# Idle products ahead of the first rows, an opening in another order, and gathered rows added by TensorE at the end

## What is computed

```python
def _L0_attn_ref(x, Wq, bq, Wkv, bkv, Wo):      # 8 query heads, one key/value head, sinusoidal positions
    scores = jnp.einsum('bhqd,bkd->bhqk', q, k) * scale
    scores = jnp.where(causal[None, None, :, :], scores, jnp.finfo(scores.dtype).min)
    probs = jax.nn.softmax(scores, axis=-1)
...
def _L0_ffn_ref(h, router_w, w1, b1, w2, b2):   # 14 experts, the best one, gelu
...
def _L1_attn_ref(x, W_in, W_delta, b_delta, W_B, W_C, A_log, D_param, W_out):
    def step(h, inp):                            # 256 channels x 16 states, over 1024 tokens
        d_t, B_t, C_t, u_t = inp
        dA = jnp.exp(d_t[..., None] * A)
        h = dA * h + d_t[..., None] * B_t[:, None, :] * u_t[..., None]
        y_t = jnp.einsum('bdn,bn->bd', h, C_t)
        return (h, y_t)
...
    y = jnp.swapaxes(ys, 0, 1) + u * D_param
    y = y * jax.nn.silu(res)
    return y @ W_out
def _L1_ffn_ref(x, gate_w, w1, w2):             # 8 experts, the best two, relu
    for e in range(NUM_EXPERTS):
        h = jax.nn.relu(jnp.einsum('bsd,fd->bsf', x, w1[e]))
        y = jnp.einsum('bsf,df->bsd', h, w2[e])
        out = out + combine[..., e, None] * y
    return out

xn = _layernorm(x, axis=-1)
x = x + _L0_attn_ref(xn, ...) + _L0_ffn_ref(xn, ...)
xn = _layernorm(x, axis=-1)
x = x + _L1_attn_ref(xn, ...) + _L1_ffn_ref(xn, ...)
```

## Time and profile before

| what | us |
|---|---|
| median of 3 runs (lowest, highest) | 730.55 (729.79, 736.21) |
| the profiled execution | 729.45 |
| its span, first to last instruction | 727.6 |
| DVE busy | 531.4 (73%) |
| TensorE busy | 636.8 (88%) |
| ScalarE busy | 417.7 (57%) |
| POOL busy | 251.3 (35%) |
| TensorE's mean granted clock | 0.958 |

### The profile page before, as it was taken

One profiled execution on the slowest core, in us unless ns is written; L12 is line 12 of the kernel. 1 busy time (PEld: TensorE's weight loads), 2 busy tenths in 40 slices (PEclk: granted clock), 3 DMA queues, 4 the chain that ended last, 5 costly groups with the idle time before them and its releaser, 6 DMA issues. The chain is left out here.

```text
span 727.6 us, 11182 instructions
## 1 busy us (share of the span) xinstructions
PE 636.8 (88%) x3414; PEld 450.1 (62%) x3414; DVE 531.4 (73%) x791; ACT 417.7 (57%) x869; POOL 251.3 (35%) x195
## 2 busy tenths in 40 slices
PE   3889999999999885988999999997788789988675
PEld 1667777777769753545566666665437778887223
DVE  5774434444445223278999999999999889999998
ACT  1365656556545354567778778875656566656310
POOL 0102212122200043000423542461115867787873
PEclk9799999999999998999999999999899999999888
DMA  8500000000059921022688998899862455554113
GB/s 278 201 5 9 12 12 7 11 7 8 26 161 294 323 58 30 1 68 61 157 201 191 219 237 218 201 228 262 196 149 80 148 150 163 153 144 117 37 43 83
DMA packets 61676, 89.99 MB, mean 124 GB/s; under 512 B 7712, under 2 KB 36256, under 8 KB 61632
## 3 DMA queue, kind: packets, MB, share of 16 engines
q1 hardware_dynamic: 41472, 57.96, 25.9%
q0 software_dynamic: 9408, 26.22, 17.3%
q10 hardware_dynamic: 10752, 5.24, 2.4%
HBM read 54.67 MB, written 14.81 MB: 95 GB/s over the span
## 5 line engine op out<-in xcount | busy, mean ns | idle before, releaser
L1645 DVE TENSOR_REDUCE nmax<-PS 128x1 f32<-128x128 f32 (+7 forms) x128 | 96.2, 751 | 110.5 <-PE PS L1046 96.0
L708 ACT COPY ROOM<-PS 128x512 f32<-128x512 f32 (+1 forms) x192 | 86.0, 484 | 101.3 <-PE PS L1058 92.0
L1074 PE MATMUL PS<-ROOM 128*128 128x512 f32 (+3 forms) x384 | 142.8, 491 | 0.5 <-ACT ROOM L708 0.5
L715 ACT ACTIVATE ROOM<-PS,nmax 128x128 f32<-128x128 f32 (+7 forms) x128 | 95.8, 749 | 30.9 <-DVE nmax L1645 28.6
L1058 PE MATMUL PS<-CST,ROOM 128*128 128x128 f32 x576 | 87.3, 280 | 12.1 <-ACT ROOM L708 10.4
L570 POOL DMA_DIRECT2D ROOM<-ROOM x32 | 28.6, 893 | 181.9 <-DVE ROOM L1744 181.9
L1058 PEld LDWEIGHTS PS<-CST,ROOM 128*128 128x128 f32 x576 | 65.8, 144 | 33.9 <-issue 26.2
L1074 PEld LDWEIGHTS PS<-ROOM 128*128 128x128 f32 x384 | 65.5, 192 | 29.9 <-issue 26.3
L1043 PE MATMUL PS<-LATER 128*128 128x512 f32 (+2 forms) x192 | 74.5, 498 | 7.4 <-ACT ROOM L715 5.9
L535 POOL DMA_INDIRECT rows_in<-XN,slot x48 | 70.8, 1474 | 27.5 <-DVE slot L1545 14.2
L549 POOL TENSOR_TENSOR QL<-ROOM,QH 128x512 fp32r<-128x512 f32 x16 | 20.6, 1287 | 155.2 <-ACT QH L683 155.2
(11 more groups left out here) (182 smaller groups left out, 1214.2 us busy)
## 6 DMA issues: line engine op xcount, KB each, us to landing
ROOM<-bc_rows SPq DMA_DIRECT2D x32, 512.0 KB, 4.2
ROOM<-ROOM POOLq DMA_DIRECT2D x32, 512.0 KB, 5.6
LATER<-in_w SPq DMA_DIRECT2D x48, 256.0 KB
ROOM<-in_w SPq DMA_DIRECT2D x32, 321.0 KB, 4.3
rows_in<-zero SPq DMA_DIRECT2D x20, 256.0 KB, 3.3
X<-GA POOLq DMA_DIRECT2D x12, 256.0 KB, 7.5
LATER<-rows_in SPq DMA_DIRECT2D x24, 128.0 KB
rows_out<-ROOM ACTq DMA_DIRECT2D x24, 128.0 KB
```

The source lines that it names most:

```text
L708: nc.scalar.copy(dst, src).then_inc(s_ed, 1)
L715: nc.scalar.activation(PR[:, s, 0:nk], sc[:, 0:nk], ACT.Exp, bias=nmax[:, i % 4:i % 4 + 1], accum_out=rsum[:, i:i + 1]).then_inc(s_ex, 1)
L1074: r = mm(PS[:, 6, lo:BANK], V[:, j, :], PT[:, 4 * group + j, lo:BANK], start=j == 0, stop=True, skip_group_check=True)
L1645: nc.vector.tensor_reduce(nmax[:, i % 4:i % 4 + 1], sc[:, 0:(i + 1) * P], AX_X, ALU.max, negate=True).then_inc(s_nm, 1)
```

## The change

1. *Opening, TensorE.* 34 bf16 products of the zero tile with itself, written to bank 0 and read by nobody (`keep_busy`), stand ahead of the first transposes. `transposes(1)` moves from after score block 0 to after block 1 and the second query.
2. *Opening, DVE and ScalarE.* The first two maxima and the second query's evacuation stand ahead of `rows_out(1)` and `values(0)`. On ScalarE the exponents of block 0 and 1 stand ahead of `take_transposed(1)`, and a one-column exponent loads the table of exponents ahead of both.
3. *Rounds 5 to 11 of the scan, POOL.* Two gathers between the quarter product and the adds, where one gather followed the adds; 18 instead of 25 remain behind the loop.
4. *End.* ScalarE multiplies each gathered tile by its weight (`weigh_rows`), two quarters ahead of the last state's decays and two behind them. DVE adds the first batch's rows in four 128x512 adds; TensorE adds the second batch's through the identity into the banks of the output product (`add_rows`), with eight idle products before the last y, and the output product accumulates on top. The second batch's gating goes by halves of the tokens, and the output product starts after the first half.

```diff
@@ SP @@
-                sp.wait_ge(*((s_gu, NT + 8 * (q + 1)) if q < 2 else (s_oe, q + 1)))
+                sp.wait_ge(*((s_gu, NT + 2 * (q + 1)) if q < 2 else (s_oe, q + 1)))
@@ POOL @@
             def add(n, c, shared=True, first=False):
-                if c == 0 and shared:
-                    quarter(n)
...
             for n in range(SHARED, LATE):
+                quarter(n)
+                if n > LATE // 2 - 2:
+                    gathers(2)
                 add(n, 0)
                 add(n, 1)
-                if n > LATE // 2 - 2:
-                    gathers(1)
             gathers(len(rows))
@@ ScalarE @@
                 query_high(0, 0)
-                take_transposed(1)
-                head(0, False, True)
+                act.wait_ge(s_zero, 1)
+                nc.scalar.activation(lnt[:, 5, 0:1], zero[:, 0:1], ACT.Exp)
+                head(0, False, True, after={1: (lambda: take_transposed(1),)})
...
-            with act.Fori(LATE, STATE) as n:
+
+            def weigh_rows(q):
+                act.wait_ge(s_g1[q], 16 * 8)
+                for k in range(2):
+                    for t in range(4):
+                        row = G1b[q // 2][:, 8 * (q % 2) + 4 * k + t, :]
+                        r = nc.scalar.activation(row, row, ACT.Copy, scale=wsel[1 + q // 2][:, k, 4 * (q % 2) + t:4 * (q % 2) + t + 1])
+                r.then_inc(s_gw, 1)
+
+            with act.Fori(LATE, STATE - 1) as n:
                 decay(n, 0)
                 decay(n, 1)
+            weigh_rows(0)
+            weigh_rows(1)
+            decay(STATE - 1, 0)
+            decay(STATE - 1, 1)
+            weigh_rows(2)
+            weigh_rows(3)
@@ TensorE @@
+            def keep_busy(at, number):
+                for _ in range(number):
+                    mm(bank(at), R3[:, 0:P], R3[:, 0:BANK], start=True, stop=True)
...
+            pe.wait_ge(s_zero, 1)
+            keep_busy(0, 34)
             pe.wait_ge(s_cst, 16)
...
                     if opening and i == 3:
+                        if not b:
+                            pe.wait_ge(s_ve, 2)
                         ranks(b)
...
-                    if isinstance(g, int) and g == 0 and i == 0:
+                    if isinstance(g, int) and g == 0 and i == 1:
                         transposes(1)
-                    if isinstance(g, int) and g == 0 and i == 1:
                         logits(1)
-                        pe.wait_ge(s_ve, 2)
...
             def scan_out(b):
-                pe.wait_ge(s_yt, 2 * b + 2)
                 if b == 0:
+                    pe.wait_ge(s_yt, 2)
...
                 for q in range(2):
+                    if b:
+                        pe.wait_ge(s_yt, 4 + 2 * q)
...
-                                   start=(k == 0), stop=(k == 1))
+                                   start=(k == 0 and not b), stop=(k == 1), skip_group_check=b > 0)
...
+            def add_rows(q):
+                pe.wait_ge(s_gw, q + 1)
+                for k in range(2):
+                    at = 8 * (q % 2) + 4 * k
+                    mm(bank(OUT_BANK[1] + q % 2), ident, GA[:, at:at + 4, :].rearrange("p t d -> p (t d)"),
+                       start=(k == 0), stop=(k == 1), skip_group_check=True)
+
+            pe.wait_ge(s_sn, 2 * STATE - 1)
+            add_rows(2)
+            keep_busy(OUT_BANK[1] + 1, 8)
             add_y(STATE - 1, 0)
             add_y(STATE - 1, 1)
+            add_rows(3)
             scan_out(1)
@@ DVE @@
                 keys_low()
-                rows_out(1)
-                values(0)
...
-                head(0, False, True, beside=steps, after={1: (route_tokens,)})
+                head(0, False, True, beside=steps, after={1: (lambda: rows_out(1), lambda: values(0), route_tokens)})
...
-            def combine_second(b):
-                for q in (2 * b, 2 * b + 1):
-                    dve.wait_ge(s_g1[q], 16 * 8)
+            def combine_second():
+                for q in range(2):
+                    dve.wait_ge(s_gw, q + 1)
+                    x = X[:, 4 * q:4 * q + 4, :]
                     for k in range(2):
                         if k:
-                            dve.wait_ge(s_gu, NT + 8 * q + 4)
-                        for t in range(4):
-                            x = X[:, 4 * q + t, :]
-                            stt(x, G1b[q // 2][:, 8 * (q % 2) + 4 * k + t, :], wsel[1 + b][:, k, 4 * (q % 2) + t:4 * (q % 2) + t + 1], x,
-                                ALU.mult, ALU.add).then_inc(s_gu, 1)
+                            dve.wait_ge(s_gu, NT + 2 * q + 1)
+                        at = 8 * q + 4 * k
+                        tt(x, G1b[0][:, at:at + 4, :], x, ALU.add).then_inc(s_gu, 1)
...
+            def gated_second():
+                for hf in range(2):
+                    sl = slice(hf * BANK, (hf + 1) * BANK)
+                    for c in range(2):
+                        dve.wait_ge(s_yp, 2 * (STATE - LATE) - 1 + c)
+                        tt(SR1[:, c, sl], bank(4 + 2 * c + hf), SR1[:, c, sl], ALU.mult).then_inc(s_yt, 1)
...
-            combine_second(0)
-            gated(1)
-            combine_second(1)
-            dve.wait_ge(s_gu, NT + 32)
+            combine_second()
+            gated_second()
             scan_out(1)
```

15 lines of the change are left out of this document (6 added, 9 removed).

## The result

The changed kernel is slower: 744.44 us, the median of four runs (742.28 to 745.11), against 733.38 us for the kernel before on the same chip (four runs, 729.79 to 736.9). The ratio is 1.0141, with a 95% interval of 1.0106 to 1.0177. That lies inside the forecast range, 2.4 us above the forecast. The profiled execution took 745.11 us, with a span of 743.3.

What follows compares the result with a forecast made beforehand. DVE was taken to limit the scan rounds at 8.57 us each, POOL following. 14.9 - 2.0 - 0.7 = +12.2 us on the profiled 729.45 gave 741.6, forecast 742, range 735 to 746.

Steps and rivals of the forecast that it cites:

- The rounds: Scan rounds: POOL's second add holds up the c = 1 scan, rounds 10.70 instead of 8.57, seven scans, +14.9 us.
- Q: Scan rounds: start of POOL's quarter product, 2.35 us after the last c = 1 scan's start; next scan due at 6.22.
- The prediction's other way for a round: Scan rounds: scan gets in first, second add stands behind it, following scan meets the first add; about 10.55 a round, +12.
- Rival 1: Scan rounds: no exclusion, second add runs beside the scan, only the gains stay, 727.8 us; chance 0.12.
- rival 2: Scan rounds: part of the collision dodged, a gather lies beside the scan, +6 to +8, 735 us; chance 0.08.
- Rival 3: Longer scan rounds: TensorE becomes the limit as its clock falls in their gaps, 1 us more for five or so, 747; chance 0.08.
- The late gathers: Behind the loop: 18 gathers instead of 25, six a round, 27.4 us from scan 12; last rows in time.
- Cost 0: Late rounds and end: ScalarE's weighting, 2.2 us a quarter, fits its waits and adds no time.
- The end: Last C product to last result add: 722.6 instead of 724.54 in the old trace's clock, -2.0 us.
- What they give is the clock, since y took 5.40: End, TensorE: eight idle products, 1.75 us, keep the clock up so the last y takes 3.6 instead of 5.40.
- The opening: Start to logits: keys in 1.8 instead of 3.75 us, normalisation 1.9 later, logits read at 29.7 to 30.1, -0.7 us.
- may fall to half clock again: Opening: TensorE waits some 3 us for the second normalisation and may drop to half clock; no separate price given.

Runs made afterwards that it cites:

- gathers_2: Kernel before, with only the two gathers between quarter product and adds in rounds 5 to 11: 732.65 us against 719.29, ratio 1.0209.
- second_add_small: Changed kernel with POOL's second add of rounds 5 to 11 cut from 1024 columns to 8: 721.21 us in its one run.
- gap_filled: Changed kernel with 14 more idle products just ahead of the second transposes: 729.58 us against 722.15 for the kernel before, ratio 1.0133.
- no_idle_at_end: Changed kernel without the eight idle products ahead of the last y: 732.53 us against 722.15 for the kernel before, ratio 1.0164.
- end_dve_last: Kernel before, gathers unmoved; ScalarE weighs three quarters, TensorE adds the third, DVE weighs and adds the last: 722.9 us against 721.3, ratio 1.0014.
- open_filled: Kernel before with the 34 idle products, the reordered opening and 14 idle products ahead of the second transposes: 719.03 us against 719.26, ratio 1.0.

## Why the prediction was right, and where it was not

**The rounds: right.** The step that POOL's adds begin at Q + 3.67 and end at Q + 8.35, and that the scan, due at Q + 6.22, waits for them, came out as Q + 3.68, Q + 8.34 and Q + 6.22. Seven rounds were touched. `gathers_2` shows the whole effect alone, and in `second_add_small` it goes when the overlap goes. The size was 14.1 instead of 14.9: the scan ended 2.16 us behind the add and not 2.27, so each round is 10.58 and not 10.70. The Trainium skill says that the order of issue decides who waits (SBUF — State Buffer, Who interferes with whom). The seven rounds agree: the second add (the later half of the row of 653.11, so from 655.44) began 0.2 us ahead of the scan, the two adds kept their 4.66, and the scan waited. The scan of 568.96 in `gap_filled` does not fit it, if the order of issue is that of the starts in the rows: it started ahead of both adds and waited for both. The prediction's other way for a round, in which the next scan meets the first add and waits for it alone, does not fit the nine such scans either: they waited for both adds. Rival 1 (no exclusion) and rival 2 (a gather beside the scan) are out by the rows: no c = 1 scan of the seven is below 4.27. (In rival 1 the prediction has the scan stay at 8.57; that is the round, the scan's own time is 2.27.) Rival 3 too: DVE waits in the rounds for POOL alone, and all rounds are alike.

**The late gathers: right.** Eighteen from 700.22 to 727.42, 27.2 us where 27.4 was counted, and in time. "Cost 0" of the weights on ScalarE holds as well, with 2.45 us a quarter instead of 2.2.

**The end: right direction, -3.7 instead of -2.0.** The mis-sized term is the clock ahead of the last y: I took over the 2.76 us of round 14's y from the earlier trace rows, partly at half clock, and so had it end 3.0 us ahead of the last C product's end; it ended 4.35 ahead (725.54 + 1.88 against 731.77). It starts 10.2 us ahead of the last C product's end in both traces, and the clock was at half until 708.0 before, but only until 725.1, 3.5 us of it, after. That is 1.35 of the 1.75 us. The rest is the pace of the y (3.44 from its start to the next, not 3.6), of the rows of quarter 3 (1.71, not 1.8) and of the output (3.73, not 3.84). There is also a wait that I had left out: the rows of quarter 2 wait for the c = 0 scan of n = 15. In the changed kernel that scan ends at 727.35 and the y at 727.42. In `gap_filled`, `second_add_small` and `no_idle_at_end`, where the y of round 14 runs at full clock throughout, TensorE waits 1.68 us for it, and the rows start 4.37 us ahead of the last C product's end in all four. A faster y could thus not have brought more. "What they give is the clock, since y took 5.40" was wrong of the eight idle products: `no_idle_at_end` had 3.70 without them. The 5.40 of before came behind a wait of 1.92 us; in `no_idle_at_end` the rows of quarter 2, added in between, leave a wait of only 1.31. That the shorter wait is why the clock stayed up is not shown.

**The opening: wrong in sign, +1.5 instead of -0.7.** The failed step is the clock behind the second query. I had written that TensorE "may fall to half clock again", but gave that no price in the likeliest case, and worked the query, the transposes and the logits through at full clock. In the changed kernel the clock was at half from 22 us on. It cost 0.5 us at the query of 21.56 (1.59 instead of 1.08), which the second normalisation stands behind, and 1.7 at the logits (3.59 instead of 1.88). The normalisation thus moved by 2.65 us (23.86 against 21.21) and not by 1.9, and the logits were read at 32.51. `gap_filled` shows that the rest of the working was right: with the clock at 1.00 the normalisation starts at 23.01, where I had 23.15, and the logits are read at 29.57, where I had 29.7 to 30.1. (Its transposes of batch 0 also start 0.3 us earlier, at 11.29 instead of 11.62.) The wait of 2.91 us, for which I had some 3, came as foreseen, but the clock had fallen ahead of it. The idle products and the reordering, taken by themselves, give -0.7 and +3.2 us at the logits.

**What was not in the sum.** The 4.1 us of the stretch between need be nothing of the change: the code there is the same, and on the other chips it is spread by more than that. That they are nothing of it is not shown by a run, but the medians have less of it: 14.1 + 1.5 - 3.7 - 0.3 = 11.6, against 11.1 between the medians on the same chip. The forecast was 12.2 more than before: the rounds came out 0.8 us cheaper, the end 1.7 and the store 0.3, and the opening 2.2 dearer. That these errors nearly cancel is luck. And the 2.4 us by which 742 misses 744.44 are in the chip's runs of the kernel before, whose median was 733.38 in the end, 2.8 us above the 730.55 that the forecast started from.

## What to carry to other kernels

Where two engines share a resource exclusively, write down each engine's cycle and the time at which each shared piece starts within it: POOL here had 8.0 us of work in a round of 8.57, one gather of 1.25 fitted behind its adds at no cost, and the same gather ahead of them cost 0.76 in each round, two of them 2.0. A chain that is made shorter at the end is only worth what its last input allows: look at when the last transfer lands, and let the engine with the least behind it take that piece (`end_dve_last` did so and had a shorter end than before, though not a time that is measurably shorter). And price a stretch of TensorE that others wait for at both clocks: the same logits took 1.85 to 2.15 us or 3.4 to 3.6, and whether the clock fell ahead of a gap, behind it or without one differed from trace to trace.

## What the runs showed of the hardware that I had not expected

- The same instructions, 0.06 us apart, were granted the full clock in one execution and half in another (22 to 24 us in `gap_filled` and `open_filled`). A single trace therefore does not price a reordering that lives by the clock: openings of the same code were spread by 1.7 to 1.8 us.
- The granted clock stands at 1.00 in the windows from 12 to 18 us of the kernel before, where its keys run at half the pace (3.75 us for what takes 1.95 in the changed kernel). So early in the span the pace of the rows says more than that column does.
- POOL's indirect gathers took 2.5 to 2.8 us instead of 0.94 where they came behind the start of an all-SBUF scan of the late rounds, so it is not POOL's arithmetic alone that this scan holds up.
- A scan that met the first of POOL's two adds waited for both, up to 7.3 us instead of 2.27, even where its row starts 0.4 us ahead of theirs.
- The last store took 4.23 us in `end_dve_last` and 2.71 to 3.05 in all others: 1.3 us saved ahead of it was 0.2 behind it. Why, I did not look into further.
